# First layer's inverse transform: row products in 32-row quarters, column products in 64-row halves, two sets of slots turned together

## What is computed

```python
def _L0_conv_ref(x, weights_r, weights_i):
    ...
    x_ft = jnp.fft.rfft2(x)
    out_ft = jnp.zeros((B, OUT_C, Nx, x_ft.shape[-1]), dtype=jnp.complex64)
    mix = lambda xs, ws: jnp.einsum('bixy,ioxy->boxy', xs, ws)
    out_ft = out_ft.at[:, :, :K2, :MODES_T].set(mix(x_ft[:, :, :K2, :MODES_T], w[0]))
    ...
    return jnp.fft.irfft2(out_ft, s=(Nx, Nt))
...
    x = x + _L0_conv_ref(_gn(x), L0_conv_weights_r, L0_conv_weights_i)
    x = x + _L1_conv_ref(_gn(x), L1_conv_gain)
    x = x + _L2_conv_ref(_gn(x), L2_conv_weight)
    x = x + _L3_conv_ref(_gn(x), L3_conv_weights)
```

## Time and profile before

| what | value |
|---|---|
| device time, median of 3 runs (lowest, highest) | 924.1 us (920.47, 928.2) |
| profiled execution, span from the first to the last instruction | 904.1 us |
| difference of the median and the span | 20.0 us |
| PE busy in the span | 755.6 us (84%) |
| DVE busy | 586.3 us (65%) |
| ACT busy | 456.1 us (50%) |
| POOL busy | 86.2 us (10%) |
| mean granted clock of PE | 0.938 |

### The profile page before, as it was taken

How to read it: one execution, slowest core, us unless ns; L and a number is a source line. 1 busy time by engine, 2 the same in 40 slices (tenths; PEclk the granted TensorE clock), 3 DMA queues, 4 the chain that set the end, 5 groups by cost and what they waited for, 6 DMA issues and landing times. The chain is left out here.

```text
span 904.1 us, 27651 instructions
## 1 busy us (share of the span) xinstructions
PE 755.6 (84%) x11429; PEld 633.2 (70%) x11429; DVE 586.3 (65%) x1097; ACT 456.1 (50%) x768; POOL 86.2 (10%) x80
## 2 busy tenths in 40 slices
PE   7999997785599667876799999958888498988996
PEld 7999996674588546665344444428777388888996
DVE  3554464777847745887786777776666676765445
ACT  0133336775343305652699995007887556775200
POOL 0000000010010002644022313000000100000000
PEclk9999998998899987997999999988999898999998
DMA  8599878862110000000000000004000447860036
GB/s 309 205 344 350 317 217 253 186 137 43 27 31 0 0 2 1 0 0 1 1 1 2 1 1 1 1 1 95 0 0 0 93 95 162 175 128 1 1 142 236
DMA packets 48668, 80.52 MB, mean 89 GB/s; under 512 B 20034, under 2 KB 38472, under 8 KB 43736
## 3 DMA queue, kind: packets, MB, share of 16 engines
q1 hardware_dynamic: 31960, 62.75, 25.0%
q10 hardware_dynamic: 16640, 16.78, 5.4%
HBM read 51.01 MB, written 27.92 MB: 87 GB/s over the span
## 5 line engine op out<-in xcount | busy, mean ns | idle before, releaser
L1588 DVE SCALAR_TENSOR_TENSOR X<-bank,c_power,X 32x512 f32 x128 | 96.8, 756 | 36.5 <-PE bank L1538 32.8
L1731 PE MATMUL bank<-m_xp,m_kf 128*32 128x64 f32 x2048 | 82.7, 248 | 22.2 <-DVE m_xp L1666 11.1
L1731 PEld LDWEIGHTS bank<-m_xp,m_kf 128*32 128x32 f32 x2048 | 81.4, 171 | 23.5 <-issue 23.5
L220 DVE BATCH_NORM_STATS2 bn<-X 128x6 f32 x128 | 83.1, 683 | 2.9 <-POOL X L1328 1.6
L420 DVE COPY ks_rows<-bank 128x512 f32<-128x512 f32 x64 | 41.2, 687 | 66.6 <-PE bank L350 66.6
L438 ACT COPY ks_spec<-bank 128x512 f32<-128x512 f32 x64 | 34.4, 589 | 97.4 <-PE bank L365 97.4
L1494 ACT ACTIVATE c_r<-X,c_nrm 32x1024 f32 (+1 forms) x56 | 74.9, 1337 | 2.4 <-DVE c_nrm L1562 1.1
L350 PE MATMUL bank<-ks_fw,ks_src 64*128 64x64 f32 x1024 | 68.7, 298 | 6.3 <-DMA ks_src<-in_L_conv_weights 6.3
L350 PEld LDWEIGHTS bank<-ks_fw,ks_src 64*128 64x128 f32 x1024 | 68.1, 215 | 6.2 <-issue 6.2
L365 PE MATMUL bank<-ks_fh,ks_rows 64*128 64x128 f32 (+1 forms) x1152 | 71.5, 279 | 0.0
L365 PEld LDWEIGHTS bank<-ks_fh,ks_rows 64*128 64x128 f32 (+1 forms) x1152 | 67.0, 183 | 2.6 <-issue 1.8
(11 more groups left out here) (183 smaller groups left out, 1683.5 us busy)
## 6 DMA issues: line engine op xcount, KB each, us to landing
ks_src<-in_L_conv_weights SPq DMA_DIRECT2D x16, 1024.0 KB, 7.0
kf<-ks_spec ACTq DMA_DIRECT2D x16, 1024.0 KB, 9.2
m_kf<-kf SPq DMA_DIRECT2D x32, 512.0 KB, 8.5
X<-in_x SPq DMA_DIRECT2D x4, 2048.0 KB, 12.6
out_y<-X SPq DMA_DIRECT2D x32, 256.0 KB, 2.6
xf<-l_y SPq DMA_DIRECT2D x24, 112.0 KB, 2.1
l_wb<-in_L_conv_weights_r SPq DMA_DIRECT2D x4, 512.0 KB, 11.5
l_wb<-in_L_conv_weights_i SPq DMA_DIRECT2D x4, 512.0 KB, 13.4
```

Of the source, the lines that this page charges most:

```text
L220: dve.bn_stats(self.bn[:, c, :], self.X[:, q, c * CH:(c + 1) * CH]).then_inc(step, 1)
L1588: dve.scalar_tensor_tensor(x, of.rearrange("p (y x) -> p y x", x=HN), filt.power[at, 2:3], x, ALU.mult, ALU.add).then_inc(added, 1)
L1731: last = pe.matmul(ps[4 * half + m // 8][at:at + C, m % 8 * N:(m % 8 + 1) * N], kf[p][:, j, :, H * half + m], xp[half][:, j, m].rearrange( ...
```

## The change

The stage gets a function of its own, `l0_inverse_stage`, for all four groups in straight code instead of a loop.

- Staging and its tile go: PE transposes y itself, two sets at a time, so 8 transposes of 128 x 128 per group instead of 16 of 128 x 64. The zero fill goes too.
- `l0_ih` holds the 56 used rows, padded to 64, twice. The column products use one half of the partitions each: 16 instructions per group as before, but of 64 rows, alternating between the halves and between two banks.
- The column matrix delivers image rows in another order, so that four neighbouring rows of `i0_rows` belong to the four quarters of the image (rows j, 16+j, 32+j, 48+j).
- `l0_iw` is the 32 x 64 block four times, one below the other (32 KB instead of 128 KB). The row products are 64 instructions per group of 32 rows by 64 columns, one per quarter and bank 4 to 7 in turn. Two steps g fill the four banks, half a group; then `pixels` counts up once.
- DVE adds four chunks in a row (0, 2, 4, 6 and then 1, 3, 5, 7), then takes their four statistics.
- PE starts a half group's rows when all four additions of the half before are done. The next group's first transposes and columns are issued among this group's rows. ACT follows in that order. There are four `i0_tt` tiles, one per step g.

```diff
-    out["l0_ih"] = np.concatenate([complex_matrix(kx, n, 1.0) / N, np.zeros((P - 2 * KX, P))])
+    quarters = complex_matrix(kx, n.reshape(4, N // 4).T.reshape(N), 1.0) / N
+    out["l0_ih"] = np.tile(np.concatenate([quarters, np.zeros((N - 2 * KX, P))]), (2, 1))
...
-    out["l0_iw"] = two(iw.reshape(2 * KT, N), 4)
+    out["l0_iw"] = np.tile(iw.reshape(2 * KT, N), (4, 1))
...
+                def turn(q):
+
+                    for u in range(HALVES):
                         for b in range(IB):
+                            m = pe.transpose(ps[u][:, b * P:(b + 1) * P],
+                                             y[:, 2 * u:2 * u + 2, :, :, IB * q + b].rearrange("p s k r -> p (s k r)"),
+                                             pr.ident[:])
                         m.then_inc(turned, 1)
...
+                def columns(q):
+
+                    pe.wait_ge(turned_read, 2 * q + 2)
+                    for u in range(HALVES):
+                        if u == 1 and q:
+                            pe.wait_ge(turned2_read, G * q)
                         for k in range(4):
+                            for s2 in range(2):
+                                at = slice(s2 * N, (s2 + 1) * N)
+                                m = pe.matmul(ps[2 * u + s2][:, k * P:(k + 1) * P],
+                                              cols[at, u, k].rearrange("p b o -> p (b o)"), mh[at], start=True, stop=True)
                         m.then_inc(made, 1)
...
+                def multiply_rows(q, g):
+
+                    pe.wait_ge(turned2_read, G * q + g + 1)
+                    n = 2 * q + g // 2
+                    if g % 2 == 0 and n:
+                        pe.wait_ge(added, 4 * n)
+                    for k in range(4):
+                        to = (g % 2 * 4 + k) * N
+                        for h in range(4):
+                            at = slice(h * C, (h + 1) * C)
+                            m = pe.matmul(ps[4 + h][:, to:to + N], tt[g][at, k * P:(k + 1) * P], mw[at],
                                           start=True, stop=True)
+                    if g % 2:
                         m.then_inc(pixels, 1)
+
+                turn(0)
+                columns(0)
+                for q in range(Q):
+                    pe.wait_ge(made_read, 4 * q + 4)
+                    turn_rows(q, 0)
+                    turn_rows(q, 1)
+                    if q + 1 < Q:
+                        turn(q + 1)
+                    multiply_rows(q, 0)
+                    turn_rows(q, 2)
+                    multiply_rows(q, 1)
+                    turn_rows(q, 3)
+                    if q + 1 < Q:
+                        columns(q + 1)
+                    multiply_rows(q, 2)
+                    multiply_rows(q, 3)
...
+                for q in range(Q):
+                    for phase in range(2):
+                        n = 2 * q + phase
+                        dve.wait_ge(pixels, n + 1)
+                        for h in range(4):
+                            c = 2 * h + phase
+                            x = pr.X[:, q, c * CH:(c + 1) * CH]
+                            dve.tensor_tensor(x, x, ps[4 + h][:], ALU.add).then_inc(added, 1)
+                        for h in range(4):
+                            dve.wait_ge(added, 4 * n + h + 1)
+                            pr.chunk_stats(dve, q, 2 * h + phase, step)
+                    pr.group_stats(dve, q, step)
...
+                copy_columns(0)
+                copy_made(0)
+                for q in range(Q):
+                    copy_rows(q, 0)
+                    copy_rows(q, 1)
+                    if q + 1 < Q:
+                        copy_columns(q + 1)
+                    copy_rows(q, 2)
+                    copy_rows(q, 3)
+                    if q + 1 < Q:
+                        copy_made(q + 1)
```

More of the change, by code:

```diff
@@ L806, in _, with l0_inverse_stage @@
                 pool.memset(y[:, :, KX:].rearrange("p s x r b -> p s (x r b)"), 0.0)
-def inverse_stage(pr, name, y, slots, modes, mats, rows4, loads, copies):
+def l0_inverse_stage(pr, y, mats, loads, copies):
     nc, ps = pr.nc, pr.psum
[L820 to L829, removed]
-    with ExitStack() as ctx:
[L831 to L835, removed]
+    HALVES = KT // 8
+    G = N // 16
+    turned, turned_read, made, made_read = (pr.sem(f"i0_{n}") for n in (
+        "turned", "turned_read", "made", "made_read"))
+    turned2, turned2_read, pixels, added, step, next_const = (pr.sem(f"i0_{n}") for n in (
+        "turned2", "turned2_read", "pixels", "added", "step", "next_const"))
+    mh, mw = mats
+    with ExitStack() as ctx:
+        cols = pr.sb(ctx, "i0_cols", [P, HALVES, 4, IB, C])
+        rows = pr.sb(ctx, "i0_rows", [P, N, KT, 2])
+        tt = [pr.sb(ctx, f"i0_tt{g}", [P, CH]) for g in range(G)]
         with nc.Block() as block:
@@ L843, in _ @@
                 sp.wait_ge(next_const, 16 * (len(loads) + len(copies)))
[L845 to L860, removed]
@@ L904, in _, with turn_rows @@
[L904 to L917 removed]
+                def turn_rows(q, g):
+                    if g >= 2:
+                        pe.wait_ge(turned2_read, G * q + g - 1)
+                    for k in range(4):
+                        m = pe.transpose(ps[2 + g % 2][:, k * P:(k + 1) * P],
+                                         rows[:, 4 * (4 * g + k):4 * (4 * g + k) + 4].rearrange("p h s r -> p (h s r)"),
+                                         pr.ident[:])
+                    m.then_inc(turned2, 1)
@@ new lines, in copy_columns, with copy_made @@
+                def copy_columns(q):
+                    for u in range(HALVES):
+                        act.wait_ge(turned, 2 * q + u + 1)
+                        act.copy(cols[:, u].rearrange("p k b o -> p b k o"),
+                                 ps[u][:].rearrange("p (b k o) -> p b k o", b=IB, k=4)).then_inc(turned_read, 1)
+                def copy_made(q):
+                    for s in range(4):
+                        act.wait_ge(made, 2 * q + s // 2 + 1)
+                        act.copy(rows[:, :, 4 * s:4 * s + 4, :].rearrange("p h s r -> p s h r"),
+                                 ps[s][:].rearrange("p (s h r) -> p s h r", s=4, r=2)).then_inc(made_read, 1)
```

88 lines of the change are left out of this document (8 added, 80 removed).

## The result

| | before | after |
|---|---|---|
| device time, median of 4 runs (lowest, highest) | 925.27 us (920.47, 928.2) | 903.61 us (899.59, 904.26) |
| profiled execution: time, span | –, 904.1 us | 903.89, 902.1 us |
| mean granted clock of PE | 0.938 | 0.915 |
| first layer's inverse, from the end of the mix on DVE | 69.6 us | 55.5 us |

The ratio after to before is 0.975 [0.971, 0.979], a gain of 21.7 us. Yet the two spans, 904.1 and 902.1, differ by only 2.0 us, and the mean clock is lower after the change. Three numbers for one edit, 21.7, 14.1 and 2.0, are what has to be explained.

The account below looks back on a forecast made before the run. PE's own queue was taken to bound the first layer's inverse. With DVE setting the period, 257.0 + 4 x 10.7 = 299.8, plus 2.2 = 302.0 against 314.0: 12.0 us less, span 892.1, time 912.1 us, range 906 to 919.

Parts of the forecast that it names:

- Bound: First layer's inverse: PE's queue sets the period before, 14.87 us per group; after the change DVE does, 10.7 against PE's 10.1.
- Row products and switches: PE, per group: 128 row records at 0.0286 us, 3.66 instead of 6.91; seven tile-size switches of 0.165, 1.15 us.
- Column products: PE, per group: 32 records of 64 rows at 0.0565 us each, 1.81 us, switches counted apart.
- Written-out code in the stage: PE's loop over groups as straight code: "issue" gaps of 0.48 us, 1.4 times per group, 0.7 us per group.
- Hand-overs and head: Between PE and DVE, gaps of 0.55 us per group, 2.2 in all; stage's head: DVE's first addition at 257.0, not 258.50.
- One sign of being wrong: Listed beforehand as showing the forecast wrong: a granted clock under 0.9 in the first layer's inverse.
- the slower rival: PE's new hand-over gaps bring half clock for the whole stage: 18.2 us per group, 20 more, 944 us; chance 0.06.
- The step that failed: Whole kernel: the 20.0 us between median 924.1 and span 904.1 were carried over unchanged, making span 892.1 into time 912.1.
- All hides: Rival: no gap reaches DVE and the clock is warm early; stage 15.3 us less, 908.8 us; chance 0.14.
- The hand-overs as the bound: Rival: PE stays the bound at the hand-overs, 11.9 us per group; 8.6 us less, 915.5 us; chance 0.20.
- by twos: Rival: row quarters overlap by twos only, 7.2 us instead of 3.66, PE 13.7 per group; 923 us; chance 0.06.

Follow-up runs that it names:

- the two other profiles: The changed kernel profiled again without edit (median 904.0 us, stage 57.4), and the changed kernel with the fourth layer left out (624.1 us, stage 58.2).
- the runs without look-ahead: Changed kernel with each group's work finished before the next group's begins: 946.54 us in one execution; with the last layer left out 648.21 us.
- the increments: Kernel before with 244 semaphore increments on PE behind the loop over groups in the first layer's inverse: 957.03 us.
- the plain order: Changed kernel, all four layers, PE and ACT finishing one group's transposes, columns and rows before the next group's: 946.54 us in one execution.
- the columns' order: Changed kernel with the four column products of one half in a row before the other half's, instead of halves in turn: 906.41 us in one execution.

## Why the prediction was right and wrong

*Bound.* PE's queue set the period before, DVE sets it now; both were as forecast. The period is 10.49 instead of 10.7, 4 x 0.21 = 0.8 us in the stage.

*Row products and switches.* Forecast: 3.66 for the products, 0.165 for each switch. Measured 4.04 for the three bursts with their three switches, against 3.66 + 3 x 0.165 = 4.16. The estimate from the speedup in the Trainium skill, TensorE: Matmul & The Clock Gate, Measured speedup vs the span model, was 4.7 without switches; the measurement, 4.04 with them, is below it and decides. 32 records take 1.05 where 32 x 0.0286 = 0.92, so 0.13 for the switch. In the Trainium skill, TensorEngine Tiling (Array Packing), Key Properties says that a change of tiling mode drains the engine; the trace agrees in that a change costs time.

*Column products.* 1.81 and a switch, 1.98; measured 2.05.

*Written-out code in the stage.* 0.7 us per group for "issue" gaps. Measured none: all idle time of PE in the steady groups ends with DVE. PE's own work per group is thus 10.49 - 0.82 - 0.41 = 9.3 instead of 10.1.

*Hand-overs and head.* 2.2 us of gaps let through; measured 0.95, once, in the last group, at the lower clock of the stage's end, 0.61; in the two other profiles 1.17 and 3.53 (2.02 and 1.51, in the last group). The head was 12.50 against 12.6, then 14.16 and 12.64. Together the stage took 55.5, 57.4 and 58.2 where the forecast had 57.6 (302.0 - 244.4): right, within what its clock does from execution to execution. One sign of being wrong did come, a granted clock under 0.9 in the stage, 0.87. It was not the fall that the slower rival meant: the steady part ran at 1.00, and the lower clock lies in the head (0.63 from 247.06 to 255.50) and at the end.

*Behind the stage* the forecast had nothing. The edge products that follow the stage's end at the lower clock take 9.97 instead of 8.86 us; smaller differences of both signs follow, and the stage began 2.7 us later in this execution. The last layer's row products begin 12.4 us earlier, against 12.0 forecast.

*The step that failed* is "the median of the runs shown, 924.1, is 20.0 above the span, and I carry these 20.0 over". Outside the span lie 1.8 to 1.9 us in the profiles of both kernels, so the remark under the table of the time before, that the 20.0 us lie around it, is wrong too. The profiled execution, at about 906 us by that, was not one of the three runs that made the median, and what it lacked was not around its span but inside: the last layer's row products at full clock all but to their end, 33.2 us, where the second profile of the same kernel has 53.2. A sum made on that execution cannot see time that only the usual ones spend, and a constant of 20.0 cannot follow when the change alters it. By the traces the usual gain is 868.12 - 853.23 = 14.9 us up to those products and 53.2 - 43.7 = 9.5 within them, 24.4 against the spans' 926.6 - 902.1 = 24.5. That the forecast still came within 8.5 us of the median is luck. For the profiled execution its terms are 912.1 - 18.2 (1.8 outside the span in place of 20.0) + 10.4 (the last layer's products, priced as unchanged) - 0.4 (ahead of them) = 903.9: two errors of opposite sign.

A second mis-sizing belongs to it: written-out code was priced only by what it costs in its stage (0.7 per group), not by what it does to PE's later code. It costs nothing in the stage and took 15.7 us off the median of the kernel before by itself. This part of the gain is not a fixed number: it depends on how many executions of the kernel before are long, and its median was 914.12, 925.75, 928.22 and 928.77 in the four later comparisons. Nor do the two effects add: 11.0 + 15.7 would be 26.7, and 21.7 and then 24.8 were measured. The two profiles of the changed kernel lose the clock part of the way (43.7 and 39.9 us), that with only the loop written out keeps it (31.1).

*The rivals.* "All hides" (908.8) came nearest in time, by the same luck; its stage, 15.3 us shorter, fits the first profile (14.1) but not the two others (12.5 and 11.4), which fit the forecast's 12.0. The hand-overs as the bound and "by twos" are refuted by the rows above. The slower rival did not happen in this kernel, but the runs without look-ahead show that such a loss is real: 13 us slower than before.

*Open.* What makes the "issue" gaps. They stand 128 product records apart, which with their weight loads are 256 instructions. In the kernel before the first one stood at record 86 in one profile and at 470 = 86 + 3 x 128 in the other. And 244 instructions more, 12 short of 256, moved it by 6 records. All this speaks for the supply of PE's code in blocks, with a head start that differs between executions, but no run shows the supply itself. Why a written-out loop changes where the gaps first stand hundreds of microseconds later is open too, and why a gap of 0.38 brought the clock down where 0.48 and 0.75 (below) did not. The place does not tell: with the first gap at record 92 the clock fell twice (the increments, the plain order), with the first at 604 = 92 + 4 x 128 it held (the columns' order). A kernel without these gaps in the last layer was not tried, nor one that keeps both gains.

## What to carry to other kernels

Compare the profiled execution's span with the times before any sum is made on it: if they differ by more than what lies around a span (1.7 to 2.8 us in all runs here), the profile shows an execution of another kind, and the difference sits in some stage. Small products on row quarters pay when neighbours alternate between quarters and other work fills PE's waits; without either, this change was a loss here. An edit that makes code longer or shorter can move the time of a stage far behind it, so measure it once with that stage left out.

## What the runs showed of the hardware

In the last layer's row products the granted clock fell from 2.4 to 1.2 GHz behind pauses of 0.38 to 0.75 us, with PE otherwise busy without a break, and did not come back in the 44 us of the window shown above, with PE busy throughout, nor when four transposes of full size were put between each 128 product records. Longer pauses were followed by it more often: over the ten profiles of kernels with all four layers, the clock fell behind one of 13 "issue" pauses of 0.20 to 0.49 us there, and behind seven of eight of 0.59 to 0.75. The length does not decide alone. PE's timeline of the first profile of before, between the rows:

```profile
884.06 3.80 PE L1053 MATMUL bank<-c_l_iw,xm 32*128 32x64 f32 x128 [0.75 <-issue]
```

128 records in 3.80 us behind a pause of 0.75: 2.4 GHz still. Behind the next pause of 0.75 in the same execution, at 896.62, it was 1.2 GHz.

A semaphore increment as an instruction of its own on PE is not free: with 244 of them DVE's wait at that place was 31.73 us where it is 1.11 without, so at least 30.6/244 = 0.13 each. The first of them ran while DVE was still at work; PE's own pause there, 36.12 us, gives at most 0.15.

Records on the same quarter and into the same bank, four products in a row, take 0.079 each and in turn 0.033 (a switch within both); on the same half 0.086 and in turn 0.064, all at 2.4 GHz. In the Trainium skill, TensorE: Matmul & The Clock Gate, The mechanism says that a weight load overlaps with products in flight only when it goes to another row group; these two runs agree.
